# Cross-attention and ternary FFN on one core: attention scores as sixteen 32-row products with a key tile two heads wide

## The chip, the cores and the metric

The kernel runs as one program on one core of a Trainium2 chip. The metric is device time in microseconds (us) of one execution; lower is better. Three executions of the kernel before took 215.14 us in the median (214.61 to 218.46).

## What is computed

x is 8 batches of 256 tokens by 256 features; the context has 8 batches of 64 keys by 64 features. The first half is cross-attention with 16 heads of 16 features:

```
n = layernorm(x)
q = n @ Wq.T;  k, v = split(ctx @ Wkv_expand.T)
scores[b,h] = q[b,h] @ k[b,h].T / sqrt(16)      # 256 queries x 64 keys
scores = where(tril(256 x 64), scores, -max)    # only queries below 64 are masked
out = softmax(scores) @ v;  x = x + out @ Wout.T
```

The second half is a gated FFN on layernorm(x): rms-normalised and rounded activations, ternary weights, `silu(x w1) * (x w2)` (1024 wide), again rounded, times w3, added to x.

## The kernel before

Each engine has its own instruction list, written by hand, and waits on semaphores; nothing reorders it. The attention of one batch b is handled in steps that the lists spread over several iterations, so that the five engines work on different batches at once. The attention part is `iteration(0)` to `iteration(6)` (3 and 4 in a hardware loop), after a preamble that loads and transposes the weights and starts batches 0 to 2; after it come 16 token blocks of the FFN.

The steps around the change, for one batch b, with the engine's name (PE is TensorE, DVE VectorE, ACT ScalarE, POOL GpSimd):

- `keys(b)`, POOL, L334: builds the tile `k_diag`. For each of two chunks c of 128 features (8 heads of 16) it holds 8 heads x 64 keys = 512 columns; column block h is the keys' features times a 0/1 mask `head_of` that leaves only head h's 16 rows. Chunk 1 of batch 0 is built by DVE instead (L1000).
- `scores(b)`, PE: two matmuls of 512 columns add the causal mask to the first 128 queries' scores (L502). Then for each half t of the queries and each chunk c one fp32 matmul of 128 rows by 512 columns (L511): `wide[n*512:...]` with n = 2t + c, one PSUM bank each. After each half it signals `scores_done`. An fp32 matmul appears in the trace as two records, so these four are x8.
- `maximum(b, t)`, DVE, L942: row maximum per head of half t, once that half's scores are signalled. `shift(b, t)`, L948: subtracts it and writes `probs`. Both read 1024 columns, two whole banks.
- ACT: exponentials of `probs` (L779); POOL: `half_sums` (L366); DVE: `sums` (L955) and the reciprocal; PE: transposes of `probs` (`probs_T`, L462), `weigh` (L536, eight fp32 matmuls on four 32-column groups of the array, x16 in the trace), `recip_T`; DVE: `divide` (L963); PE: `project` (L555); DVE: `residual` (L969).

`qT` (the projected queries, features on partitions) and `kT` have features in the order of `Wq` and `Wkv_expand`, which PE transposes at the start (`square_T`, and the four wkv transposes).

Orders that the prediction speaks of. DVE in iteration j: `sums(j)`, `divide(j-1)`, `measure(j+3)`, `maximum(j+1, 0)`, ..., `residual(j-1)`, `maximum(j+1, 1)`, two `shift(j+1)`. PE in iteration j: `scores(j+1)`, `probs_T(j, 0)`, from j = 3 `tokens_T(j-3)` (L615, transposes of the FFN's quantised tokens, which ACT writes in L819), `project(j-1)`, `probs_T(j, 1)`, `query(j+2)`, `weigh(j)`, `recip_T(j)`, `normT(j+3)`. In the preamble PE has `values_of(0)`, `values_of(2)`, `scores(0)`, `values_of(4)`, `values_of(6)` (L477), `normT(1)` (L462), `query(1)`, and then the sum of the weights' magnitudes (L663) that DVE waits for.

Of the kernel before, what the change touches and what calls it, by code (L numbers as in the profile page):

```python
# [19 lines left out]
bf16 = mybir.dt.bfloat16  # L20
i16 = mybir.dt.int16
ALU = mybir.AluOpType
ACT = mybir.ActivationFunctionType
AX = mybir.AxisListType

P = 128
# [10 lines left out]
def need(engine, semaphore, value):  # L37

    if isinstance(value, int) and value <= 0:
        return  # L40
    engine.wait_ge(semaphore, value)


def build_program(nc, x_d, ctx_d, wq_d, wkv_d, wout_d, w1_d, g1_d, w2_d, g2_d, w3_d, g3_d, out_d):
    B, S, D = x_d.shape
    SK, L = ctx_d.shape[1:]
    H = w1_d.shape[0]
    NH = 16
    HD = D // NH
    TB = S // P  # L50
    DC = D // P
    HC = H // P
    HPC = NH // DC
    PR = HPC // 2
# [6 lines left out]
    with stack:  # L61
        def sb(name, shape, dt=fp32):
            return stack.enter_context(nc.sbuf_tensor(name, shape, dt))
# [4 lines left out]
        def sem(name):  # L68
            return stack.enter_context(nc.semaphore(name))
# [3 lines left out]
        wq_in = sb("wq_in", [P, DC, D])  # L73
        wout_in = sb("wout_in", [P, DC, D])
        wkv_in = sb("wkv_in", [P, 2 * DC, L])
# [5 lines left out]
        ident_h = sb("ident_h", [P, P], bf16)  # L81
        ones = sb("ones", [P, P])
        mask_h = sb("mask_h", [P, HPC, SK], bf16)
        head_of = sb("head_of", [P, HPC])
        key_half = sb("key_half", [P, 2])
        wqT = sb("wqT", [P, DC, D])
# [3 lines left out]
        kT = sb("kT", [P, DC, B * SK])  # L90
        v_all = sb("v_all", [P, B, D])
        k_diag = sb("k_diag", [P, DC, HPC, SK])
        v_pair = sb("v_pair", [P, 2 * PR, 2, HD])
# [10 lines left out]
        qT = sb("qT", [P, DC, S])  # L104
        row_max = sb("row_max", [P, TB, NH])
# [40 lines left out]
            "scores_done", "max_ready", "shifted", "probs_ready", "sums_ready", "recip_ready"))  # L146
        recip_wide, kp0_ready, half_ready = sem("recip_wide"), sem("kp0_ready"), sem("half_ready")
        pT_done, pT_ready, pv_done, rT_done, rT_ready, attnT_ready = map(sem, (
# [102 lines left out]
        with nc.Block() as block:  # L251
# [32 lines left out]
            def _(pool):  # L284
# [19 lines left out]
                g.affine_select(out=mask_h[:], in_=mask_h[:], compare_op=ALU.is_ge, fill=MASKED, base=0,  # L304
                                pattern=[[0, HPC], [-1, SK]], channel_multiplier=1).then_inc(const_set, 1)

# [22 lines left out]
                def keys(b):  # L329

                    need(pool, scores_done, 2 * b)

                    for c in range(1 if isinstance(b, int) and b == 0 else DC):
                        last = g.tensor_tensor(  # L334
                            out=k_diag[:, c, :, :],
                            in0=kT[:, c, bass.ds(b * SK, SK)].unsqueeze(1).to_broadcast([P, HPC, SK]),
                            in1=head_of[:].unsqueeze(2).to_broadcast([P, HPC, SK]), op=ALU.mult)
                    last.then_inc(kp_ready, 1)

# [10 lines left out]
                norm(0)  # L350
                pool.wait_ge(kT_set, 2)
                keys(0)
                pool.wait_ge(v_set, 1)
# [106 lines left out]
            def _(pe):  # L460
                def transpose(out, in_, n=P):
                    return nc.tensor.matmul(out, in_, ident[0:n, 0:n], is_transpose=True, start=True, stop=True)  # L462

                pe.wait_ge(ident_set, 1)

                def square_T(bank_, w):

                    for kc in range(DC):
                        for oc in range(DC):
                            last = transpose(bank_[:, (kc * DC + oc) * P:(kc * DC + oc + 1) * P],  # L470
                                             w[:, oc, kc * P:(kc + 1) * P])
                    return last
# [25 lines left out]
                def scores(b):  # L498

                    need(pe, shifted, 2 * b)  # L500
                    for c in range(DC):
                        nc.tensor.matmul(wide[:, c * 512:(c + 1) * 512], ident_h[:], mask_h[:],  # L502
                                         start=True, stop=False)
                    need(pe, qT_ready, b + 1)
                    need(pe, kp_ready, b + 1)
                    if isinstance(b, int) and b == 0:
                        pe.wait_ge(kp0_ready, 1)
                    for t in range(TB):
                        for c in range(DC):
                            n = t * DC + c  # L510
                            last = nc.tensor.matmul(wide[:, n * 512:(n + 1) * 512], qT[:, c, t * P:(t + 1) * P],  # L511
                                                    k_diag[:, c, :, :], start=(t == 1), stop=True)
                        last.then_inc(scores_done, 1)

# [65 lines left out]
                pe.wait_ge(wq_ld, 16)  # L580
                square_T(bank7, wq_in).then_inc(wqT_done, 1)
                keep_warm(5)
# [5 lines left out]
                pe.wait_ge(wkv_ld, 16)  # L588
                for n in range(2 * DC):
                    last = transpose(wide[0:L, n * P:(n + 1) * P], wkv_in[:, n, :])  # L590
# [150 lines left out]
            def _(act):  # L741
# [14 lines left out]
                def query_copy(b):  # L756
                    need(act, q_done, b + 1)
                    need(act, scores_done, 2 * b)
                    a.copy(qT[:].rearrange("p c s -> p (c s)"), bank5[:]).then_inc(qT_ready, 1)
# [158 lines left out]
            def _(dve):  # L918
# [17 lines left out]
                def by_head(ap, t):  # L936

                    return ap[:].rearrange("p (t n k) -> p t n k", t=TB, k=SK)[:, t, :, :]

                def maximum(b, t):  # L940
                    need(dve, scores_done, 2 * b + t + 1)
                    v.tensor_reduce(out=row_max[:, t, :], in_=by_head(wide, t), op=ALU.max,  # L942
                                    axis=AX.X).then_inc(max_ready, 1)

                def shift(b, t):
                    need(dve, max_ready, 2 * b + t + 1)
                    need(dve, pT_done, 4 * b - 2 + 2 * t if not isinstance(b, int) or b else 0)
                    v.tensor_tensor(probs[:, t, :].rearrange("p (n k) -> p n k", k=SK), by_head(wide, t),  # L948
                                    row_max[:, t, :].unsqueeze(2).to_broadcast([P, NH, SK]),
                                    ALU.subtract).then_inc(shifted, 1)  # L950
# [25 lines left out]
                def weights_T_copy(i, half):  # L976
# [4 lines left out]
                dve.wait_ge(ident_set, 1)  # L981
                v.tensor_copy(ident_h[:], ident[:]).then_inc(cast_set, 1)
                dve.wait_ge(x0_in, 16)
                measure(0)
# [12 lines left out]

                dve.wait_ge(const_set, 3)
                dve.wait_ge(kT_set, 2)
                v.tensor_tensor(k_diag[:, 1, :, :], kT[:, 1, 0:SK].unsqueeze(1).to_broadcast([P, HPC, SK]),  # L1000
                                head_of[:].unsqueeze(2).to_broadcast([P, HPC, SK]), ALU.mult).then_inc(kp0_ready, 1)

# [308 lines left out]
```

## Time and profile before

| | |
|---|---|
| median of 3 executions | 215.14 us (214.61 to 218.46) |
| profiled execution: span from first to last instruction (the only time shown for it) | 215.0 us |
| DVE busy | 184.2 us (86%) |
| PE busy | 170.9 us (79%) |
| ACT busy | 152.4 us (71%) |
| POOL busy | 143.6 us (67%) |
| mean granted TensorE clock | 0.959 of full speed |

The profile comes from one profiled execution. Its busy times add up what each engine was occupied; a PE record's end is modelled, so that successive records overlap, and a busy PE need not be one at its peak. The granted clock has two levels here: 1.00 is 2.4 GHz, 0.50 is 1.2 GHz. A timeline row gives the start, the time covered and, in brackets, how long the engine sat idle before the row and which engine, tile and line ended the idle time. Idle time counts only where the idle engine is the one that the end waits for.

### The profile page before, as it was taken

How to read it: one execution, taken by the hardware profiler on the slowest of the kernel's cores; microseconds unless marked ns; L12 is line 12 of the kernel's file. 1: busy time of each engine (PE TensorE's matmuls, PEld its weight loads, DVE VectorE, ACT ScalarE, POOL GpSimd, SP SyncE). 2: the span in 40 equal slices, each digit the busy share in tenths (PEclk: the TensorE clock that was granted, in tenths of full speed). 3: DMA queues.
4: the chain of work that ended last, by engine and by line, in shares of the span. 5: the costliest groups of instructions: out<-in, count | busy, mean ns of one | idle time of the engine just before them, and what ended most of it. 6: DMA issues, size and time to landing. Idle time of an engine off the chain costs nothing.

```text
span 215.0 us, 3666 instructions
## 1 busy us (share of the span) xinstructions
PE 170.9 (79%) x1073; PEld 110.0 (51%) x1080; DVE 184.2 (86%) x338; ACT 152.4 (71%) x218; POOL 143.6 (67%) x229
## 2 busy tenths in 40 slices
PE   4799877998997998999948878447489978788372
PEld 4755545585674865747436545124236544454251
DVE  2359799599999899997995889799999999999981
ACT  2355888958665896859864998829499968877622
POOL 5216292555667696886461666879899999999640
PEclk9999999999999999999997999959969999999979
DMA  6999000000000000000000000000000100010011
GB/s 163 340 377 361 27 3 2 0 2 5 0 0 3 0 0 0 0 0 3 2 0 0 0 3 0 0 2 0 30 24 24 49 24 24 24 52 24 24 49 49
DMA packets 8798, 9.09 MB, mean 42 GB/s; under 512 B 1488, under 2 KB 8400, under 8 KB 8784
## 3 DMA queue, kind: packets, MB, share of 16 engines
q1 hardware_dynamic: 8512, 8.65, 12.4%
q10 hardware_dynamic: 272, 0.26, 0.4%
q8 instruction: 7, 0.11, 0.2%
q14 instruction: 7, 0.06, 0.1%
HBM read 6.82 MB, written 2.10 MB: 41 GB/s over the span
## 4 chain that ended last, share of the span: by engine, by line
DVE 38%; issue 21%; PE 16%; ACT 12%; POOL 10%; DMA 2%; DVEq 1%; POOLq 0%; ACTq 0%
DVE hh L1195 5%; DVE probs L948 4%; DVE c_max L1213 4%; ACT q_x L819 4%; POOL u L384 4%; PE bank L555 3%; PE wide L511 3%; DVE m_x L1066 3%; DVE u_max L1059 3%; PE bank L706 2%; POOL half_sum L366 2%; DVE row_sum L955 2%; ACT hT L880 2%; DVE row_max L942 2%; PE bank L494 2%
## 5 line engine op out<-in xcount | busy, mean ns | idle before, releaser
L687 PE MATMUL wide<-wT,xqT 128*128 128x512 bf16 x128 | 33.5, 406 | 5.7 <-DVE hh L1195 3.5
L404 POOL TENSOR_TENSOR c_h<-hh,g3b 128x1024 f32<-128x1024 f32 x15 | 35.4, 2361 | 2.9 <-DVE hh L1195 2.5
L511 PE MATMUL wide<-k_diag,qT 128*128 128x512 f32 x64 | 28.9, 595 | 0.3 <-DVE k_diag L1000 0.3
L875 ACT ACTIVATE sq_junk<-hh,root_x 128x1024 bf16<-128x1024 f32 x16 | 18.4, 1147 | 15.2 <-DVE hh L1195 15.2
L706 PE MATMUL bank<-wT,hT 128*128 128x256 bf16 x128 | 17.6, 283 | 11.8 <-ACT hT L880 11.8
L334 POOL TENSOR_TENSOR k_diag<-kT,head_of 128x512 f32<-128x512 f32 x15 | 15.4, 1045 | 12.6 <-DVE kT L996 7.3
L819 ACT ACTIVATE q_x<-u,round_c,qs_x 128x256 f32<-128x256 f32 x32 | 16.6, 590 | 9.4 <-issue 5.1
L384 POOL TENSOR_TENSOR u<-xc,g 128x512 f32<-128x512 f32 x16 | 20.3, 1290 | 4.4 <-ACT q_x L819 4.4
L687 PEld LDWEIGHTS wide<-wT,xqT 128*128 128x128 bf16 (+1 forms) x128 | 12.3, 102 | 20.6 <-issue 7.3
L366 POOL TENSOR_TENSOR half_sum<-probs 128x512 f32<-128x512 f32 x16 | 20.1, 1277 | 3.4 <-ACT probs L779 3.3
L706 PEld LDWEIGHTS bank<-wT,hT 128*128 128x128 bf16 x128 | 11.6, 100 | 20.5 <-ACT hT L880 16.8
L764 ACT COPY probsT<-bank 128x512 f32<-128x512 f32 x32 | 17.1, 588 | 6.7 <-PE bank L462 6.5
L880 ACT ACTIVATE hT<-bank,round_c 128x1024 bf16<-128x1024 int16 x16 | 17.6, 1100 | 4.4 <-PE bank L615 4.4
L942 DVE TENSOR_REDUCE row_max<-wide 128x16 f32<-128x1024 f32 x16 | 19.5, 1217 | 0.9 <-PE wide L511 0.5
L1195 DVE TENSOR_TENSOR hh<-gate,wide 128x1024 f32<-128x1024 f32 x16 | 19.4, 1210 | 0.1
L1213 DVE TENSOR_REDUCE c_max<-c_h 128x1 f32<-128x1024 f32 x16 | 19.3, 1208 | 0.0
L511 PEld LDWEIGHTS wide<-k_diag,qT 128*128 128x128 f32 x64 | 12.0, 190 | 13.5 <-issue 12.2
L948 DVE TENSOR_TENSOR probs<-wide,row_max 128x1024 f32<-128x1024 f32 x16 | 18.7, 1213 | 0.0
L462 PE MATMUL bank<-ident,probs 128*128 128x128 f32 x128 | 16.7, 273 | 2.2 <-ACT probsT L764 1.4
L462 PEld LDWEIGHTS bank<-ident,probs 128*128 128x128 f32 x128 | 14.8, 142 | 7.0 <-issue 6.1
L869 ACT ACTIVATE gate<-wide,dq_x 128x1024 f32<-128x1024 f32 x16 | 17.8, 1110 | 0.4 <-PE wide L687 0.4
L555 PE MATMUL bank<-woutT,attnT 128*128 128x256 f32 x64 | 17.0, 414 | 0.7 <-DVE attnT L963 0.7
(139 smaller groups left out, 385.8 us busy)
## 6 DMA issues: line engine op xcount, KB each, us to landing
w_in<-in_L_ffn_w SPq DMA_DIRECT2D x3, 1024.0 KB, 10.3
out<-y SPq DMA_DIRECT2D x16, 128.0 KB, 1.7
x_sb<-in_x SPq DMA_DIRECT2D x1, 1280.0 KB, 12.4
x_sb<-in_x SPq DMA_DIRECT2D x1, 512.0 KB, 5.3
g3b<-in_L_ffn_g SPq DMA_DIRECT2D x1, 512.0 KB, 7.9
wq_in<-in_L_xattn_Wq ACTq DMA_DIRECT2D x1, 256.0 KB, 4.0
x_sb<-in_x SPq DMA_DIRECT2D x1, 256.0 KB, 3.6
wout_in<-in_L_xattn_Wout SPq DMA_DIRECT2D x1, 256.0 KB, 12.2
```

The costliest lines, as they stand in the source:

```text
L366: last = g.tensor_tensor(out=half_sum[:, t, :, :], in0=e[:, :, 0, :], in1=e[:, :, 1, :], op=ALU.add)
L384: last = g.tensor_tensor(out=u[:, t, :, :], in0=xc[:, t, :].unsqueeze(1).to_broadcast([P, 2, D]), in1=g12[:], op=ALU.mult)
L404: g.tensor_tensor(out=c_h[:, t, :], in0=hh[:, t, :], in1=g3b[:], op=ALU.mult).then_inc(c_ready, 1)
L462: return nc.tensor.matmul(out, in_, ident[0:n, 0:n], is_transpose=True, start=True, stop=True)
L511: last = nc.tensor.matmul(wide[:, n * 512:(n + 1) * 512], qT[:, c, t * P:(t + 1) * P], k_diag[:, c, :, :], start=(t == 1), stop=True)
L687: last = nc.tensor.matmul(wide[:, (w * 2 + n) * 512:(w * 2 + n + 1) * 512], xqT_cols(T, w * DC + c), w_cols[:, 4 * n:4 * n + 4, c, :], sta ...
L706: last = nc.tensor.matmul(down_banks[t][:, 0:D], hT[:, t, n, :], w_cols[:, n, :, :], start=(n == 0), stop=(n == HC - 1))
L819: last = a.activation(q_x[:, t, w, :], u[:, t, w, :], ACT.Identity, scale=qs_x[:, t, w:w + 1], bias=round_c[:, 0:1])
L942: v.tensor_reduce(out=row_max[:, t, :], in_=by_head(wide, t), op=ALU.max, axis=AX.X).then_inc(max_ready, 1)
L948: v.tensor_tensor(probs[:, t, :].rearrange("p (n k) -> p n k", k=SK), by_head(wide, t), row_max[:, t, :].unsqueeze(2).to_broadcast([P, NH, ...
L1195: v.tensor_tensor(hh[:, t, :], gate[:, t, :], wide[:, H:2 * H], ALU.mult).then_inc(hh_ready, 1)
L1213: v.tensor_reduce(out=c_max[:, t:t + 1], in_=c_h[:, t, :], op=ALU.max, axis=AX.X, apply_absolute_value=True).then_inc(cm_ready, 1)
```

## The change

The scores of one batch become sixteen fp32 matmuls instead of four. The features of `Wq` and of the keys' part of `Wkv_expand` are permuted while they are transposed (`by_chunk`), so that the 32 rows of row group r in chunk c hold heads 4r + 2c and 4r + 2c + 1. Each matmul takes 32 rows of one group, 128 queries and 128 columns (2 heads x 64 keys), and writes to bank r; the four that follow each other use the four row groups and four banks. The key tile `k_pair` needs a 0/1 mask for two heads only (`half_of`, built once by DVE), and has 2 x 128 columns instead of 2 x 512. It is built by one POOL instruction a batch, also for batch 0, where the DVE instruction L1000 goes. The mask of the scores goes to four banks with 256 columns each. Each bank now holds both halves t, so `scores_done` is signalled once, after all sixteen, and `maximum(b, 0)` waits for that; the waits of `query_copy` and `keys` on it are counted accordingly. `maximum` and `shift` read a half as four pieces of 256 columns in the four banks, again 1024 columns.

```diff
@@ keys (POOL)
-                    need(pool, scores_done, 2 * b)
-
-                    for c in range(1 if isinstance(b, int) and b == 0 else DC):
-                        last = g.tensor_tensor(
-                            out=k_diag[:, c, :, :],
-                            in0=kT[:, c, bass.ds(b * SK, SK)].unsqueeze(1).to_broadcast([P, HPC, SK]),
-                            in1=head_of[:].unsqueeze(2).to_broadcast([P, HPC, SK]), op=ALU.mult)
-                    last.then_inc(kp_ready, 1)
+                    need(pool, scores_done, b)
+                    g.tensor_tensor(
+                        out=k_pair[:], in0=kT[:, :, bass.ds(b * SK, SK)].unsqueeze(2).to_broadcast([P, DC, 2, SK]),
+                        in1=half_of[:].unsqueeze(1).unsqueeze(3).to_broadcast([P, DC, 2, SK]),
+                        op=ALU.mult).then_inc(kp_ready, 1)
@@ transposes of wq and wkv (PE)
+                def by_chunk(ap, block):
+
+                    at = ap.rearrange("p (c r k) -> p r c k", c=DC, k=2 * HD)
+                    return at[:, block * PR // DC:(block + 1) * PR // DC, :, :]
...
@@ scores (PE)
-                    for c in range(DC):
-                        nc.tensor.matmul(wide[:, c * 512:(c + 1) * 512], ident_h[:], mask_h[:],
-                                         start=True, stop=False)
+                    for r in range(PR):
+                        nc.tensor.matmul(wide[:, r * 512:r * 512 + 2 * P], ident_h[:], mask_h[:],
+                                         start=True, stop=True)
                     need(pe, qT_ready, b + 1)
                     need(pe, kp_ready, b + 1)
-                    if isinstance(b, int) and b == 0:
-                        pe.wait_ge(kp0_ready, 1)
                     for t in range(TB):
                         for c in range(DC):
-                            n = t * DC + c
-                            last = nc.tensor.matmul(wide[:, n * 512:(n + 1) * 512], qT[:, c, t * P:(t + 1) * P],
-                                                    k_diag[:, c, :, :], start=(t == 1), stop=True)
-                        last.then_inc(scores_done, 1)
+                            for r in range(PR):
+                                rows, at = slice(32 * r, 32 * r + 32), r * 512 + (t * DC + c) * P
+                                last = nc.tensor.matmul(wide[:, at:at + P], qT[rows, c, t * P:(t + 1) * P],
+                                                        k_pair[rows, c, :, :], start=(t == 1), stop=True,
+                                                        skip_group_check=True)
+                    last.then_inc(scores_done, 1)
@@ maximum and shift (DVE)
-                    return ap[:].rearrange("p (t n k) -> p t n k", t=TB, k=SK)[:, t, :, :]
+                    return ap[:].rearrange("p (r t n k) -> p r t n k", r=PR, t=TB, k=SK)[:, :, t, :, :]
...
-                    need(dve, scores_done, 2 * b + t + 1)
+                    need(dve, scores_done, b + 1)
@@ DVE, preamble
+                dve.wait_ge(const_set, 3)
+                v.tensor_reduce(out=half_of[:], in_=head_of[:].rearrange("p (r h) -> p h r", h=2), op=ALU.add,
+                                axis=AX.X).then_inc(half_of_set, 1)
...
-                dve.wait_ge(const_set, 3)
-                dve.wait_ge(kT_set, 2)
-                v.tensor_tensor(k_diag[:, 1, :, :], kT[:, 1, 0:SK].unsqueeze(1).to_broadcast([P, HPC, SK]),
-                                head_of[:].unsqueeze(2).to_broadcast([P, HPC, SK]), ALU.mult).then_inc(kp0_ready, 1)
```

On PE, in the preamble from the first values to the second ones, the order of instructions before (the last numbers are an instruction's rows by columns):

```order
L477 MATMUL bank<-wkvT,ctxT 128x256 x4
L502 MATMUL wide<-mask_h,ident_h 128x512 x2
L511 MATMUL wide<-k_diag,qT 128x512 x4
L477 MATMUL bank<-wkvT,ctxT 128x256 x4
L462 MATMUL bank<-ident,nrm 128x128 x4
```

and in the change:

```order
L480 MATMUL bank<-wkvT,ctxT 128x256 x4
L505 MATMUL wide<-mask_h,ident_h 128x256 x4
L513 MATMUL wide<-k_pair,qT 128x128 x16
L480 MATMUL bank<-wkvT,ctxT 128x256 x4
L461 MATMUL bank<-ident,nrm 128x128 x4
```

The place of the scores in the list is the same, here and in every iteration; two masks and four products have become four and sixteen, with as many columns in all for the masks (1024) and for the products (2048).

On DVE, the start of its list, before:

```order
L982 CAST ident_h<-ident 128x128
L927 BN_STATS ln_bn<-x_sb 128x6 x2
L933 BN_AGGR ln_mv<-ln_bn 128x2 x2
L988 TENSOR_SCALAR wqT<-bank 128x512
L991 COPY ctxT<-bank 64x1024
L994 COPY wkvT<-wide 64x512
L996 COPY kT<-wide 128x512
L1000 TENSOR_TENSOR k_diag<-kT,head_of 128x512
L1005 COPY v_all<-bank 128x512 x2
```

and in the change:

```order
L991 CAST ident_h<-ident 128x128
L993 TENSOR_REDUCE half_of<-head_of 128x2
L932 BN_STATS ln_bn<-x_sb 128x6 x2
L938 BN_AGGR ln_mv<-ln_bn 128x2 x2
L1000 TENSOR_SCALAR wqT<-bank 128x512
L1003 COPY ctxT<-bank 64x1024
L1006 COPY wkvT<-wide 64x512
L1008 COPY kT<-wide 128x512
L1013 COPY v_all<-bank 128x512 x2
```

The key instruction between the copy of the keys and the copies of the values is gone; a reduction to two columns stands near the start.

## Rows read from the trace of the kernel before

**Rows 1.** The page: busy time, share of the span and instructions by engine.

```profile
PE 170.9 (79%) x1073; PEld 110.0 (51%) x1080; DVE 184.2 (86%) x338; ACT 152.4 (71%) x218; POOL 143.6 (67%) x229
```

**Rows 2.** Groups by line: busy us, mean ns of one; idle before, releaser.

```profile
L511 PE MATMUL wide<-k_diag,qT 128*128 128x512 f32 x64 | 28.9, 595 | 0.3 <-DVE k_diag L1000 0.3
L942 DVE TENSOR_REDUCE row_max<-wide 128x16 f32<-128x1024 f32 x16 | 19.5, 1217 | 0.9 <-PE wide L511 0.5
L1213 DVE TENSOR_REDUCE c_max<-c_h 128x1 f32<-128x1024 f32 x16 | 19.3, 1208 | 0.0
L334 POOL TENSOR_TENSOR k_diag<-kT,head_of 128x512 f32<-128x512 f32 x15 | 15.4, 1045 | 12.6 <-DVE kT L996 7.3 <-PE wide L511 5.1
L344 POOL TENSOR_TENSOR v_pair<-v_all,key_half 128x256 f32<-128x256 f32 x8 | 4.9, 618 | 12.6 <-PE bank L536 11.4 <-DVE v_all L1005 1.2
```

**Rows 3.** Timeline of the preamble, all engines: start us, us covered.

```profile
13.47 1.89 PE L477 MATMUL bank<-wkvT,ctxT 64*128 64x256 f32 x8
14.44 1.04 POOL L334 TENSOR_TENSOR k_diag<-kT,head_of 128x512 f32<-128x512 f32 x1 [7.29 <-DVE kT L996]
14.47 1.56 DVE L1000 TENSOR_TENSOR k_diag<-kT,head_of 128x512 f32<-128x512 f32 x1
15.95 1.27 DVE L1005 COPY v_all<-bank 128x512 f32<-128x512 f32 x2
16.18 3.67 PE L511 MATMUL wide<-k_diag,qT 128*128 128x512 f32 x8 [0.28 <-DVE k_diag L1000]
18.26 0.19 POOL L320 TENSOR_TENSOR ln_ve<-ln_mv,ln_eps 128x2 f32<-128x2 f32 x1 [0.94 <-DVE ln_mv L933]
19.78 1.99 PE L477 MATMUL bank<-wkvT,ctxT 64*128 64x256 f32 x8
19.82 1.09 ACT L748 ACTIVATE nrm<-x_sb,ln_nb,ln_rstd 128x256 f32<-128x256 f32 x2 [1.77 <-POOL ln_nb L327]
21.03 2.35 DVE L948 TENSOR_TENSOR probs<-wide,row_max 128x1024 f32<-128x1024 f32 x2
21.70 0.66 PE L462 MATMUL bank<-ident,nrm 128*128 128x128 f32 x4
25.43 0.16 DVE L1031 TENSOR_SCALAR w_s<-bank 128x3 f32<-128x3 f32 x1 [1.39 <-PE bank L663]
```

**Rows 4.** Windows, iterations 2 and 4: length, busy PE, PEld, DVE, ACT, POOL, PEclk, ...

```profile
56.70:70.75 14.05, 12.35 (x82) 8.54 (x82) 13.64 (x28) 8.68 (x15) 9.94 (x14) 1.00 0.01 1
83.86:96.55 12.69, 11.76 (x73) 8.11 (x74) 12.27 (x26) 9.94 (x17) 9.69 (x15) 1.00 0.00 0
```

**Rows 5.** Timeline of iterations 1 and 3: PE, ACT, DVE.

```profile
40.45 3.60 PE L511 MATMUL wide<-k_diag,qT 128*128 128x512 f32 x8
44.70 1.22 DVE L942 TENSOR_REDUCE row_max<-wide 128x16 f32<-128x1024 f32 x1
67.36 3.60 PE L511 MATMUL wide<-k_diag,qT 128*128 128x512 f32 x8
69.36 2.07 ACT L819 ACTIVATE q_x<-u,round_c,qs_x 128x256 f32<-128x256 f32 x4 [2.42 <-DVE qs_x L1087]
74.23 0.69 DVE L969 TENSOR_TENSOR x_sb<-bank,x_sb 128x512 f32 x1 [0.67 <-PE bank L555]
```

**Rows 6.** Timeline, PE: the column-group products of one batch (`weigh`).

```profile
89.11 1.07 PE L536 MATMUL bank<-probsT,v_pair 128*32 128x256 f32 x16
```

**Rows 7.** Windows around 112 us (columns as above), and timeline of two projects.

```profile
108.50:111.90 3.40, 0.78 (x8) 0.47 (x8) 3.19 (x14) 2.46 (x5) 1.51 (x2) 1.00 0.00 0
111.90:115.30 3.40, 3.23 (x8) 2.60 (x9) 1.25 (x2) 2.22 (x4) 1.69 (x2) 0.50 0.00 0
...
84.63 1.95 PE L555 MATMUL bank<-woutT,attnT 128*128 128x256 f32 x8
112.07 3.58 PE L555 MATMUL bank<-woutT,attnT 128*128 128x256 f32 x8 [0.67 <-DVE attnT L963]
115.69 0.69 DVE L969 TENSOR_TENSOR x_sb<-bank,x_sb 128x512 f32<-128x512 f32 x1 [2.54 <-PE bank L555]
```

More of the change, by code:

```diff
@@ L82, in build_program @@
         ones = sb("ones", [P, P])
-        mask_h = sb("mask_h", [P, HPC, SK], bf16)
+        mask_h = sb("mask_h", [P, 2 * DC, SK], bf16)
         head_of = sb("head_of", [P, HPC])
+        half_of = sb("half_of", [P, 2])
         key_half = sb("key_half", [P, 2])
@@ L91, in build_program @@
         v_all = sb("v_all", [P, B, D])
-        k_diag = sb("k_diag", [P, DC, HPC, SK])
+        k_pair = sb("k_pair", [P, DC, 2, SK])
         v_pair = sb("v_pair", [P, 2 * PR, 2, HD])
@@ L146, in build_program @@
             "scores_done", "max_ready", "shifted", "probs_ready", "sums_ready", "recip_ready"))
-        recip_wide, kp0_ready, half_ready = sem("recip_wide"), sem("kp0_ready"), sem("half_ready")
+        recip_wide, half_of_set, half_ready = sem("recip_wide"), sem("half_of_set"), sem("half_ready")
         pT_done, pT_ready, pv_done, rT_done, rT_ready, attnT_ready = map(sem, (
@@ L304, in _ @@
                 g.affine_select(out=mask_h[:], in_=mask_h[:], compare_op=ALU.is_ge, fill=MASKED, base=0,
-                                pattern=[[0, HPC], [-1, SK]], channel_multiplier=1).then_inc(const_set, 1)
+                                pattern=[[0, 2 * DC], [-1, SK]], channel_multiplier=1).then_inc(const_set, 1)
                 g.affine_select(out=head_of[:], in_=head_of[:], compare_op=ALU.is_ge, fill=0.0, base=0,
@@ L351, in _ @@
                 pool.wait_ge(kT_set, 2)
+                pool.wait_ge(half_of_set, 1)
                 keys(0)
@@ L464, in _, with square_T @@
                 pe.wait_ge(ident_set, 1)
-                def square_T(bank_, w):
+                def by_chunk(ap, block):
+                    at = ap.rearrange("p (c r k) -> p r c k", c=DC, k=2 * HD)
+                    return at[:, block * PR // DC:(block + 1) * PR // DC, :, :]
+                def square_T(bank_, w, place=lambda ap, block: ap[:, block * P:(block + 1) * P]):
                     for kc in range(DC):
                         for oc in range(DC):
-                            last = transpose(bank_[:, (kc * DC + oc) * P:(kc * DC + oc + 1) * P],
-                                             w[:, oc, kc * P:(kc + 1) * P])
+                            last = transpose(place(bank_[:, kc * D:(kc + 1) * D], oc), w[:, oc, kc * P:(kc + 1) * P])
                     return last
@@ L580, in _ @@
                 pe.wait_ge(wq_ld, 16)
-                square_T(bank7, wq_in).then_inc(wqT_done, 1)
+                square_T(bank7, wq_in, by_chunk).then_inc(wqT_done, 1)
                 keep_warm(5)
@@ L588, in _ @@
                 pe.wait_ge(wkv_ld, 16)
-                for n in range(2 * DC):
+                for n in range(DC):
+                    transpose(by_chunk(wide[0:L, 0:D], n), wkv_in[:, n, :])
+                for n in range(DC, 2 * DC):
                     last = transpose(wide[0:L, n * P:(n + 1) * P], wkv_in[:, n, :])
@@ L757, in query_copy @@
                     need(act, q_done, b + 1)
-                    need(act, scores_done, 2 * b)
+                    need(act, scores_done, b)
                     a.copy(qT[:].rearrange("p c s -> p (c s)"), bank5[:]).then_inc(qT_ready, 1)
@@ L936, in by_head, with by_pair @@
                 def by_head(ap, t):
-                    return ap[:].rearrange("p (t n k) -> p t n k", t=TB, k=SK)[:, t, :, :]
+                    return ap[:].rearrange("p (r t n k) -> p r t n k", r=PR, t=TB, k=SK)[:, :, t, :, :]
+                def by_pair(ap):
+                    return ap.rearrange("p (r n) -> p r n", r=PR)
                 def maximum(b, t):
-                    need(dve, scores_done, 2 * b + t + 1)
-                    v.tensor_reduce(out=row_max[:, t, :], in_=by_head(wide, t), op=ALU.max,
+                    need(dve, scores_done, b + 1)
+                    v.tensor_reduce(out=by_pair(row_max[:, t, :]), in_=by_head(wide, t), op=ALU.max,
                                     axis=AX.X).then_inc(max_ready, 1)
@@ L947, in shift @@
                     need(dve, pT_done, 4 * b - 2 + 2 * t if not isinstance(b, int) or b else 0)
-                    v.tensor_tensor(probs[:, t, :].rearrange("p (n k) -> p n k", k=SK), by_head(wide, t),
-                                    row_max[:, t, :].unsqueeze(2).to_broadcast([P, NH, SK]),
+                    v.tensor_tensor(probs[:, t, :].rearrange("p (r n k) -> p r n k", r=PR, k=SK), by_head(wide, t),
+                                    by_pair(row_max[:, t, :]).unsqueeze(3).to_broadcast([P, PR, 2 * DC, SK]),
                                     ALU.subtract).then_inc(shifted, 1)
```

## The prediction

> **What bounds the kernel now.** I read the busy shares first: DVE is the fullest engine, 184.2 of 215.0 us, and PE follows with 170.9 [rows 1]. A share is an average, so the windows come next. In iterations 2 and 4 of the attention DVE is busy 13.64 of 14.05 us and 12.27 of 12.69, and PE, whose records overlap, 12.35 and 11.76 [rows 4]. The reader is to see there that what shortens an iteration is DVE work, or a wait of DVE; PE time counts only where DVE waits for PE. The groups by line tell where it does: DVE's row maxima had 0.5 us of idle before them that ended with the scores, in the whole run, and the scores cost PE 28.9 us [rows 2]. So nearly all of the scores' time lies beside DVE work. In the iterations, the other wait of DVE on PE is for `project`: 0.67 us in iteration 3 [rows 5] and 2.54 us in iteration 6 [rows 7].
>
> The preamble is different. There the engines wait for each other in a chain that passes through the scores of batch 0: PE's scores end at 19.85 us, the second values (1.99 us) run until 21.77, and `normT(1)`, ready since ACT's normalisation ended at 20.91, goes behind them at 21.70. DVE waits 1.39 us, until 25.43, for the weights' sum, and that sum comes from ACT and PE work behind `normT(1)` [rows 3].
>
> **The scores on PE.** An L511 record streams 512 columns; eight take 3.60 us, of which the last one's length is 0.59 [rows 2, 5], so a record's pace is (3.60 - 0.59) / 7 = 0.43 us, and 0.107 us for 128 columns. The change has 32 records of 128 columns, the same 4096 columns in all. How fast they go on four row groups the trace doesn't show. Bounds: one after another, 32 x 0.107 = 3.4 us and a last record's tail, no gain; four at a time, a quarter, 0.86 us, and a tail. The nearest row is `weigh`: 16 records of 256 columns, again 4096, on four column groups take 1.07 us [rows 6]. I take that, and 0.2 us more for twice as many, shorter records and for changing from whole-array to row-group products: **1.3 us** a batch, 2.3 less than now. The masks cover 1024 columns as before: nothing.
>
> The Trainium skill (page "TensorE: Matmul & The Clock Gate", Part 3) gives 3.07 times for four 32-row groups with 512 columns. By that the stage would be 3.6 / 3.07 = 1.17 us, an estimate from the page; no row of this trace has row groups.
>
> **The preamble.** DVE no longer builds half the key tile: 1.56 us go [rows 3]. It goes straight to the two value copies, 1.27 us, but the second must wait for PE's values, which end at 15.36, so the copies end near 16.1 instead of 17.2, and the statistics of batch 1 are ready near 17.1, 1.1 us earlier. POOL's one key instruction writes 256 columns; `v_pair` with as many takes 0.618 us [rows 2], so it is ready at 14.44 + 0.62 = 15.06. PE is through with values at 15.36 and with the masks near 15.95; the scores start there, only 0.2 us earlier than now, and end near 17.3 instead of 19.85. The second values end at 19.3. `normT(1)` then waits no more for PE: POOL's norm (18.26 to 19.79 before) and ACT's 1.09 us [rows 3] start 1.1 us earlier, so it starts at 19.8 instead of 21.70. That is 1.9 us. I count **1.8 us**, since some copies sit between. Behind it come the last magnitude sum on ACT, the weights' sum on PE, the query copy and exponentials of batch 0, half sums and row sums, each released by the one before, so the whole attention starts 1.8 us earlier. DVE must be ready too: maxima from 17.4 (instead of two starts with a wait between), shifts done at 21.9 instead of 23.38: it is. `half_of` is a small reduction in DVE's idle start: nothing.
>
> **The iterations.** The maxima wait for the whole batch, not for a half. Behind `maximum(j+1, 0)` on DVE stand `residual(j-1)`, the second maximum and both shifts, so a wait there would be paid in full. But the scores end ahead: in iteration 1 at 44.05, with all eight records, and the first maximum starts at 44.70; in iteration 3 at 70.96 (67.36 + 3.60) [rows 5]. With 1.3 us the reserve grows to about 3 us. The wait costs nothing, and its cover is gone only when the stage takes over 4.2 us.
>
> What do 2.3 us less of PE give? In iteration 3, `project(2)` stands behind the transposes of tokens, and those behind ACT's quantising, which ends at 69.36 + 2.07 = 71.43. PE comes to them after the scores, which end at 70.96, and eight transposes of `probs`, so later than ACT; then it would be there first and wait for ACT. Project and residual gain between nothing and the 0.67 us that DVE waits [rows 5]; I take 0.4, a little over the middle, because the last token transposes still stand behind 71.43. In iterations 4 and 5 the tokens already set the start of project, in 6 the quotient from DVE does (the row of project at 112.07 names it [rows 7]): nothing. **0.4 us** in all. POOL's keys go from 2 x 1.045 to about 0.62 us, 1.47 us less a batch [rows 2]. POOL isn't full in the windows (9.94 and 9.69 us [rows 4]), and next in its list it waits for statistics from DVE: nothing. `maximum` and `shift` read as many columns; DVE's reduction with 16 results (1217 ns) costs 9 ns more than one with a single result (1208 ns) [rows 2], so the shape of a pattern is worth at most 32 x 0.01 = 0.3 us, which I leave to the range. The FFN is not touched.
>
> **Sum:** 215.0 - 1.8 - 0.4 = 212.8 us of span. The median of the runs shown is 0.1 us above that span, so **212.9 us**, 1.0% less. A measurement of this kernel tells a change from none at about 2%, or 4.3 us. This case has 60%, and its own range is 211.8 to 214.0.
>
> **Rivals.**
> - *The row groups don't overlap* (17%). Each record needs its own weights, 128 columns wide; `weigh` loads 32 columns [rows 6] and doesn't show that wide loads go beside each other. Then scores(0) ends near 15.95 + 3.5 = 19.5, `normT(1)` gains 0.3 us, iteration 3 nothing: 214.8 us. The Trainium skill (same page, section "LDWEIGHTS (loading the stationary operand)") has a load's time go by its columns, rows not counting; 32 loads one after another would be 32 x 128 / 1.2 ns = 3.4 us, an estimate, and lead to this case.
> - *A lower clock* (13%). At 111.9 us the granted clock fell to 0.50 (1.2 GHz) after a stretch in which PE had been busy 0.78 of 3.40 us; project then took 3.58 us instead of 1.95, and DVE waited 2.54 us for it [rows 7]. Shorter scores leave PE idle about 2 us ahead of the tokens in iterations 4 and 5. If the clock falls there too, each costs about 1.6 us: 214.5 to 216.1.
> - *Slower: weight loads that nothing hides* (6%). If a record can't start before its own load ends, the pace goes from 0.107 to, say, twice that (load and stream alike): 32 x 0.214 = 6.9 us, 3.3 more than now. The point from which it decides is 4.2 us a batch, 0.13 us a record, where the first maximum in iteration 1 starts to wait. Beyond it DVE pays 3.3 us less a reserve of 0.65 to 1.2 in each of iterations 1 to 3, I guess 2 us in the later ones together, and the preamble 3: 7 + 2 + 3 = 12, so 227 us. Against it: L511's loads, as wide, are started under the running record, with no gap in the pace.
> - *More than forecast* (4%): DVE instructions held up by POOL's (L1000 took 1.56 us for what POOL did in 1.04 [rows 3]) get shorter as POOL has less to do, in the iterations too; up to 3 us more: 209.8.
>
> The range of 8 in 10 takes in the first case, the second and most of the third: 211.5 to 216.0. Faster by over 2%: the last case and a bit, 0.05. Slower by over 2%: the unhidden loads and several falls of the clock, 0.08. Within 2%: 0.87.
>
> **What the profile after would show.** The new L513 group: 32 records in about 1.3 us a batch if the groups overlap (10 us in all instead of 28.9), 3.5 if not. `normT(1)` near 19.8 us, the weights' sum on DVE near 23.6 instead of 25.43. The first maximum without idle time that the scores end. Iterations as long as before (14.0 and 12.7 us), with PE idle in place of scores. Wrong would be: a maximum that waits for L513; iterations shorter by more than 0.5 us each, which would say that PE, not DVE, bounds them; or stretches at clock 0.50 before 100 us.

## The result, and the profile after

The changed kernel takes 220.35 us in the median of 4 executions (218.69 to 221.42), the kernel before beside it 214.88 (214.60 to 218.46). The ratio is 1.026, with a 95% interval of 1.019 to 1.032: slower. All ratios here are of the executions that lie within about 1.5% of their kernel's fastest. I had forecast 212.9 us, 211.5 to 216.0. Only three executions of the kernel before stand in this ratio (214.60 to 215.14). In 75 later ones, on the chips of the experiments, it took 214.34 to 219.88 us, 217.35 in the median. Against those the change's four are about 3 us slower, not 5.5: that it is slower holds, the size of the loss is less sure than the interval says. The profiled execution's span is 219.6 us, 4.6 more than before.

The page of the changed kernel: busy time by engine, and the granted clock in 40 slices.

```profile
PE 166.0 (76%) x1288; PEld 115.3 (53%) x1288; DVE 182.7 (83%) x338; ACT 152.8 (70%) x218; POOL 132.3 (60%) x222
PEclk9998888999999995896975999758889999999955
```

The same line of the kernel before:

```profile
PEclk9999999999999999999997999959969999999979
```

The groups of the new lines (busy us, mean ns of one, idle before):

```profile
L513 PE MATMUL wide<-k_pair,qT 32*128 32x128 f32 x256 | 9.4, 283 | 0.1
L513 PEld LDWEIGHTS wide<-k_pair,qT 32*128 32x128 f32 x256 | 7.9, 186 | 1.9 <-issue 1.5 <-ACT qT L764 0.4
L333 POOL TENSOR_TENSOR k_pair<-kT,half_of 128x256 f32<-128x256 f32 x8 | 4.9, 614 | 7.3 <-DVE kT L1008 7.3
```

The scores cost 9.4 us of PE in all instead of 28.9 [rows 2], the key tiles 0.614 us each: both as priced. What the reader is to see are the two lines of the clock. In the kernel before it stays up from the start-up to 111.9 us [rows 7]; now windows of half a microsecond show it lowered from 20.7, 30.9, 82.1, 99.2 and 112.8 us on, and in the FFN. Stretches at 0.50 before 100 us were what the prediction had named as a sign of being wrong.

The changed kernel's timeline in the preamble:

```profile
15.74 1.17 PE L513 MATMUL wide<-k_pair,qT 32*128 32x128 f32 x32
16.85 1.99 PE L480 MATMUL bank<-wkvT,ctxT 64*128 64x256 f32 x8
19.73 0.66 PE L461 MATMUL bank<-ident,nrm 128*128 128x128 f32 x4 [0.89 <-ACT nrm L753]
21.06 3.48 PE L497 MATMUL bank<-nT,wqT 128*128 128x256 f32 x8 [0.68 <-ACT nT L759]
24.77 0.16 DVE L1039 TENSOR_SCALAR w_s<-bank 128x3 f32<-128x3 f32 x1 [2.50 <-PE bank L668]
```

`normT(1)` starts at 19.73 instead of 21.70 [rows 3], where I had put it at 19.8. But `query(1)` then takes 3.48 us; before, the same eight records took 1.99. Of 2.0 us gained 0.66 are left at the weights' sum (24.77 against 25.43).

Windows of the changed kernel (length, then busy PE, PEld, DVE, ACT, POOL, the granted clock third from last): for two of the falls the stretch before it, and the one at the low clock behind it.

```profile
17.00:20.60 3.60, 2.49 (x12) 1.68 (x12) 3.60 (x4) 2.23 (x5) 1.85 (x5) 1.00 1.12 356
20.80:24.00 3.20, 2.94 (x7) 2.40 (x8) 1.46 (x3) 2.11 (x3) 0.00 (x0) 0.50 0.36 138
77.50:82.00 4.50, 2.68 (x45) 2.02 (x42) 4.13 (x12) 2.44 (x5) 3.59 (x6) 1.00 0.00 0
82.20:88.90 6.70, 6.11 (x24) 5.02 (x25) 4.49 (x10) 4.11 (x8) 3.19 (x7) 0.50 0.00 0
```

And the kernel before in the same stretch of iteration 4:

```profile
77.50:82.00 4.50, 4.45 (x21) 2.58 (x19) 4.36 (x13) 2.84 (x4) 3.67 (x6) 1.00 0.00 0
```

PE was busy 4.45 of 4.50 us there before, 2.68 now, and the clock goes to 0.50 (1.2 GHz). The timeline of the changed kernel shows what that costs:

```profile
82.42 0.60 PE L620 MATMUL bank<-ident_h,q_x 128*128 128x128 bf16 x4 [2.06 <-ACT q_x L824]
83.80 3.73 PE L558 MATMUL bank<-woutT,attnT 128*128 128x256 f32 x8
87.69 0.69 DVE L978 TENSOR_TENSOR x_sb<-bank,x_sb 128x512 f32 x1 [2.05 <-PE bank L558]
101.55 0.69 DVE L978 TENSOR_TENSOR x_sb<-bank,x_sb 128x512 f32<-128x512 f32 x1 [2.20 <-PE bank L558]
```

The time that the shorter scores give back turns up as 2.06 us of idle PE in front of the tokens' transposes. `project` then runs at half the clock, 3.73 us instead of 1.95 [rows 7], and DVE waits 2.05 us for it, in an iteration in which it had not waited for it at all. In iteration 5 the wait is 2.20 us where it was 1.13, in iteration 6 2.75 (2.54 before [rows 7]).

By the starts of DVE's row sums (batches 0, 4, 5, 6, 7), and of the last gated product of the FFN, the 4.6 us come about like this:

| | before | after | difference |
|---|---|---|---|
| row_sum 0 | 30.26 | 29.75 | -0.5 |
| row_sum 4 | 82.33 | 81.33 | -1.0 |
| row_sum 5 | 95.02 | 96.06 | +1.0 |
| row_sum 6 | 109.87 | 112.19 | +2.3 |
| row_sum 7 | 124.23 | 126.87 | +2.6 |
| last hh (L1195, L1203) | 200.94 | 203.50 | +2.6 |
| end | 215.0 | 219.6 | +4.6 |

The last 2.0 us are the tail: there the clock is at 0.50 from 208.4 us on, and `down` takes 1.89 us, twice:

```profile
210.89 1.89 PE L711 MATMUL bank<-wT,hT 128*128 128x256 bf16 x8 [1.21 <-ACT hT L885]
214.84 1.89 PE L711 MATMUL bank<-wT,hT 128*128 128x256 bf16 x8 [1.21 <-ACT hT L885]
```

Before, one of the last three took 1.89 and two 1.05. The FFN's code is unchanged, and PE is idle in the same places; when the clock falls there differs between executions. The profile of e9 below, a run with the FFN and the scores of the kernel before, has such a tail too: clock 0.50 from 206.8 us on, `down` at 1.89 us in its last two places, and 15.7 us from the last hh to the end, where the two kernels above have 14.1 and 16.1. So a tail like this needs no change in the scores, and these 2.0 us are not shown to be the change's.

### The profile page after: what moved, and what is told of

Its sections match the earlier page's. It is cut to its first block, busy times and chain, and to the rows that moved or that the text cites. A ratio compares the mean times of both kernels' runs of the same rounds, so it can differ in the third digit from the quotient of the medians.

```text
span 219.6 us, 4080 instructions
## 1 busy us (share of the span) xinstructions
PE 166.0 (76%) x1288; PEld 115.3 (53%) x1288; DVE 182.7 (83%) x338; ACT 152.8 (70%) x218; POOL 132.3 (60%) x222
## 4 chain that ended last, share of the span: by engine, by line
DVE 37%; PE 18%; issue 18%; ACT 13%; POOL 10%; DMA 2%; DVEq 1%; POOLq 0%; ACTq 0%
PE bank L558 6%; DVE hh L1203 5%; POOL u L383 5%; DVE probs L957 4%; DVE c_max L1221 4%; ACT q_x L824 4%; DVE u_max L1067 4%; PE bank L497 3%; DVE m_x L1074 3%; PE bank L461 3%; PE bank L711 2%; DVE row_sum L964 2%; DVE xc L1061 2%; ACT hT L885 2%; DVE fb_bn L1048 2%
## 5 line engine op out<-in xcount | busy, mean ns | idle before, releaser
L692 PE MATMUL wide<-wT,xqT 128*128 128x512 bf16 x128 | 34.1, 411 | 4.5 <-DVE hh L1203 3.1
L711 PE MATMUL bank<-wT,hT 128*128 128x256 bf16 x128 | 18.4, 292 | 12.0 <-ACT hT L885 12.0
L558 PE MATMUL bank<-woutT,attnT 128*128 128x256 f32 x64 | 20.3, 473 | 3.2 <-DVE attnT L972 3.2
L824 ACT ACTIVATE q_x<-u,round_c,qs_x 128x256 f32<-128x256 f32 x32 | 16.6, 590 | 8.7 <-DVE qs_x L1095 4.5
L461 PE MATMUL bank<-ident,probs 128*128 128x128 f32 x128 | 20.5, 311 | 1.7 <-ACT nT L759 1.0
L461 PEld LDWEIGHTS bank<-ident,probs 128*128 128x128 f32 x128 | 17.4, 163 | 5.1 <-issue 3.1
L1203 DVE TENSOR_TENSOR hh<-gate,wide 128x1024 f32<-128x1024 f32 x16 | 19.4, 1211 | 0.1
L321 POOL TENSOR_TENSOR ln_ve<-ln_mv,ln_eps 128x2 f32<-128x2 f32 x8 | 1.6, 194 | 29.7 <-DVE ln_mv L938 29.7
L558 PEld LDWEIGHTS bank<-woutT,attnT 128*128 128x128 f32 x64 | 14.3, 235 | 6.4 <-DVE attnT L972 4.2
L497 PE MATMUL bank<-nT,wqT 128*128 128x256 f32 x64 | 16.8, 409 | 0.7 <-ACT nT L759 0.7
```

Source lines behind the costliest of these rows:

```text
L497: last = nc.tensor.matmul(bank5[:, oc * S:(oc + 1) * S], wqT[:, kc, oc * P:(oc + 1) * P], nT[:, kc, :], start=(kc == 0), stop=(kc == DC - 1))
L558: last = nc.tensor.matmul(bank4[:, t * D:(t + 1) * D], attnT[:, c, t * P:(t + 1) * P], woutT[:, c, :], start=(c == 0), stop=(c == DC - 1))
L692: last = nc.tensor.matmul(wide[:, (w * 2 + n) * 512:(w * 2 + n + 1) * 512], xqT_cols(T, w * DC + c), w_cols[:, 4 * n:4 * n + 4, c, :], sta ...
L711: last = nc.tensor.matmul(down_banks[t][:, 0:D], hT[:, t, n, :], w_cols[:, n, :, :], start=(n == 0), stop=(n == HC - 1))
L824: last = a.activation(q_x[:, t, w, :], u[:, t, w, :], ACT.Identity, scale=qs_x[:, t, w:w + 1], bias=round_c[:, 0:1])
L1203: v.tensor_tensor(hh[:, t, :], gate[:, t, :], wide[:, H:2 * H], ALU.mult).then_inc(hh_ready, 1)
```

## The experiments

All are compared with the kernel before in executions on the same chip; the changed kernel itself was not run again beside them, so that a ratio here and its 1.026 come from different sets. Theory: the idler PE loses its clock, and each fall makes longer what runs in it. Rivals: the row groups or the banks, the wait for the whole batch, or POOL and DVE in each other's way.

**More PE work in front of the scores (e1_mask7).**

```diff
-                    for r in range(PR):
+                    for r in list(range(PR)) * 7:
                         nc.tensor.matmul(wide[:, r * 512:r * 512 + 2 * P], ident_h[:], mask_h[:],
```

> The changed kernel with each batch's four mask products issued seven times over (24 more whole-array products of 256 bf16 columns, the same values written again; about 2.6 us of PE work a batch, as much as the change took away). Theory (the clock): the row-group products are fine, 1.17 us a batch; what is lost comes from stretches at clock 0.50 that the idler PE brings. Then the mean clock goes back from 0.89 to 0.95 or more and the time from 220.35 to about that of the kernel before or a little less, 212.5 to 215. Rival (the work): the loss lies in the new order of waits or in POOL and DVE work getting into each other's way; then 2.6 us more of PE work a batch gives nothing back, and the time stays at 219 to 222. Rival (the kind of work): row-group products themselves lower the clock; then it stays below 0.93 too.

Measured: ratio to the kernel before 1.002 (0.998 to 1.007), span 215.4 us, clock 0.966, no fall before 112 us:

```profile
PEclk9999999999999999999997999979969999999979
```

With 2.6 us of useless work more a batch the changed kernel takes 217.23 us in the median of 12, where it had taken 220.35, and the loss against the kernel before is gone. It is not faster than the kernel before: in the preamble the masks stand in the chain, the scores of batch 0 start at 19.05 us instead of 15.74, and row_sum 0 at 30.63.

**The same with row-group work (e2_rowpass3).** Before the masks, the sixteen products run twice with `start=True`; their results are overwritten.

```diff
+                    def products(extra):
...
+                    products(True)
+                    products(True)
                     for r in range(PR):
                         nc.tensor.matmul(wide[:, r * 512:r * 512 + 2 * P], ident_h[:], mask_h[:],
                                          start=True, stop=True)
...
+                    last = products(False)
```

> The changed kernel with the sixteen row-group products of a batch issued three times (two passes whose results are overwritten, then masks and the real pass): 2.3 us more PE work a batch, all of it in 32-row products. Theory (the clock goes by how much PE works, whatever the rows): like the kernel with seven masks, mean clock 0.95, 212.5 to 216 us. Rival (row-group products count for less than whole-array ones): the clock stays near 0.90 and the time at 218 us or more, since this one has the same time of work as the seven masks but in 32-row pieces.

Measured: 0.992 (0.987 to 0.997), span 214.0, clock 0.959, no fall before 111 us. So 32-row products on four groups hold the clock too; the rival on their kind falls. Row sums start 0.7 to 1.0 us ahead of the kernel before all through the attention: what is left of the preamble's gain.

**Shorter scores without row groups (e3_bf16).** The kernel before with scores of lower precision:

```diff
-        k_diag = sb("k_diag", [P, DC, HPC, SK])
+        k_diag = sb("k_diag", [P, DC, HPC, SK], bf16)
...
-        qT = sb("qT", [P, DC, S])
+        qT = sb("qT", [P, DC, S], bf16)
```

> The kernel before with qT and k_diag in bf16, so that the scores lose precision: four whole-array products of 512 columns at one pass each, about 0.9 us a batch instead of 3.6, with the old banks, the old wide key tile and the old signals. Theory (an idler PE lowers the clock): it falls in the iterations as in the changed kernel, mean clock about 0.90, and the time is 217 to 221 us although PE has 2.7 us less to do a batch. Rival (the fault lies in row groups, banks or the wait for the whole batch): the clock stays at 0.95 and the time is 212 to 214.5.

Measured: 1.020 (1.013 to 1.028), span 219.0, clock 0.905: slower, like the change. Its page and its iteration 4:

```profile
PEclk9998585999999997896975999957969999999969
80.65 1.03 PE L511 MATMUL wide<-k_diag,qT 128*128 128x512 bf16 x4
...
85.28 0.58 PE L615 MATMUL bank<-ident_h,q_x 128*128 128x128 bf16 x4 [2.07 <-ACT q_x L819]
86.67 2.98 PE L555 MATMUL bank<-woutT,attnT 128*128 128x256 f32 x8
89.81 0.69 DVE L969 TENSOR_TENSOR x_sb<-bank,x_sb 128x512 f32 x1 [1.29 <-PE bank L555]
```

Old banks, old key tile, old signals, and the same picture: short scores, 2.07 us idle, `project` at 2.98 us, DVE waiting. So the loss needs neither the row groups nor the new banks, key tile or signals. Its place is another in part, though: e3's clock is at 0.50 from 20.5 to 27.3 us and from 30.7 to 37.6, twice as long as the change's first two falls, and its row sums of batches 0 and 1 start 1.5 and 2.4 us later than before, that of batch 7 4.0 us later.

**The wait alone (e4_wait_both).**

```diff
-                    need(dve, scores_done, 2 * b + t + 1)
+                    need(dve, scores_done, 2 * b + 2)
```

> The kernel before in which the first maximum also waits for the second half of the scores; nothing else is changed. Theory: outside batch 0 the scores end at least 0.6 us before the first maximum starts, so 214.9 us, within 0.3%; batch 0's maxima come 1.4 us later, but DVE waits there later for the weights' sum anyway. Rival (the wait for a whole batch costs the change its time): each iteration longer by 0.5 us or more, 218 to 220.

Measured: 0.999 (0.993 to 1.005), span 214.9, the row sums where they were. No cost of the wait for the batch shows, even with the long scores. (In e4's preamble DVE waits 0.27 us for the weights' sum instead of 1.39, which takes up the later maxima, as expected.)

**Filling the idle time itself.** The filler is a whole-array product of 256 bf16 columns into a bank that PE overwrites next. In the preamble:

```diff
+                fill(bank6[:, 0:2 * P], 8)
                 normT(1)
+                fill(bank5[:, 0:2 * P], 6)
                 query(1)
...
                         pe.wait_ge(inv_ready, 1)
+                        fill(bank6[:, 0:2 * P], 20)
                         normT(2)
```

and in the iterations:

```diff
                     probs_T(j, 0)
+                    if from_(j, 1):
+                        need(pe, rT_ready, j)
+                        fill(bank5[:, 0:2 * P], 24 if isinstance(j, int) and j == 6 else 14 if from_(j, 3) else 11)
```

> The changed kernel with idle PE time filled in the preamble only (34 whole-array products of 256 bf16 columns before normT(1), query(1) and normT(2), into banks that these then overwrite). Theory (idle PE lowers the clock, and each fall costs what runs in it): no fall before 80 us, query(1) back from 3.48 to 2.0 us, row sums of batch 0 at 28.3 instead of 29.75 us; the falls at 82, 99 and 113 us stay. 1.4 us less than the changed kernel: 218 to 220 us in the same company. Rival (the falls follow the row-group products): falls near 21 and 31 us stay.

> The changed kernel with the idle time of iterations 1 to 6 filled, behind probs_T(j, 0), where PE waits for ACT's tokens or DVE's quotient (11 products of 256 bf16 columns in iterations 1 and 2, 14 in 3 to 5, 24 in 6). Theory: the falls at 82, 99 and 113 us go, DVE's waits for project in iterations 4 to 6 go back from 2.05, 2.20 and 2.75 us to 0, 1.1 and 0.9, together 3.5 us or more less than the changed kernel: 215 to 217 us. Rival (the fill is in the way, since PE has no room before project): iterations as long as in the changed kernel.

> The changed kernel with both fills, preamble and iterations. Theory: the two effects add up, 4.9 us or more less than the changed kernel, 1.5 to 2.5 us less than the kernel before; clock 0.95 or more, falls only in the FFN. Rival: the preamble's gain is lost again in the iterations, no better than with the iterations' fill alone.

| | ratio (95%) | median of all | span | clock | row_sum 0 | row_sum 7 |
|---|---|---|---|---|---|---|
| before | 1 | 217.32 (23) | 215.0 | 0.959 | 30.26 | 124.23 |
| after, in its own set | 1.026 (1.019 to 1.032) | 220.35 (4) | 219.6 | 0.889 | 29.75 | 126.87 |
| e5, preamble | 1.005 (1.000 to 1.010) | 217.44 (12) | 214.4 | 0.943 | 28.86 | 123.75 |
| e6, iterations | 0.983 (0.975 to 0.992) | 215.68 (6) | 211.4 | 0.966 | 28.88 | 120.72 |
| e7, both | 0.984 (0.977 to 0.990) | 212.74 (6) | 212.3 | 0.965 | 29.01 | 120.86 |

e5 has no fall before 94 us, e7 none before 136. In e6's profile the first fall comes at 29.7 us instead of 20.7, behind `query(1)`, so it got the preamble's gain without a fill there, with the preamble's code of the changed kernel. In the profiles the effects do not add up, against what I had expected of e7. Over all executions they differ: e6's ratio rests on three of six, and the other three took 218.17 to 220.78 us with a mean clock of 0.915 to 0.943, and no profile shows where the clock fell in them; e7's six took 212.35 to 215.35, at 0.965 or more. So only e7's gain is there each time.

e5 did better than I expected, and for a reason that the theory lacks. I had the fall at 82 us stay; it is gone, though PE is idle in iteration 4 as long as in the changed kernel:

```profile
81.51 0.40 PE L627 MATMUL bank<-ident_h,q_x 128*128 128x128 bf16 x4 [2.06 <-ACT q_x L832]
82.73 1.95 PE L563 MATMUL bank<-woutT,attnT 128*128 128x256 f32 x8
```

`project` runs at the full clock and DVE does not wait for it; the falls come at 94.6 and 108.3 us. So an idle stretch of 2.06 us is followed by a fall in one profile and not in another, and what decides it is left open. e7's profile: its clock, and iterations 4 and 6:

```profile
PEclk9999999999999999999999999859979999999978
79.45 1.69 PE L480 MATMUL bank<-mask_h,ident_h 128*128 128x256 bf16 x14
...
82.89 1.95 PE L563 MATMUL bank<-woutT,attnT 128*128 128x256 f32 x8
110.29 1.99 PE L563 MATMUL bank<-woutT,attnT 128*128 128x256 f32 x8 [0.67 <-DVE attnT L983]
112.32 0.69 DVE L989 TENSOR_TENSOR x_sb<-bank,x_sb 128x512 f32<-128x512 f32 x1 [0.96 <-PE bank L563]
```

Fourteen products lie in what had been idle time, `project` takes 1.95 us again, DVE does not wait in iteration 4 and waits 0.96 us instead of 2.54 in iteration 6. This version beats both kernels: 212.74 us in the median of 6, beside 217.32 for the kernel before.

**A third of the fill (e10_fill_half):** e7 with 4, 5 and 8 products in place of 11, 14 and 24.

> The changed kernel with the preamble's fill and a third of the iterations' fill (4 products in iterations 1 and 2, 5 in 3 to 5, 8 in 6). Theory (the clock asks for a certain amount of work, and a little of it may be missing): between the preamble's fill alone and the full fill; a fall near 109 us stays, those near 82 and 95 us may go: 214 to 217 us. Rival (any products at all in the gap hold the clock): as fast as with the full fill.

Measured: 1.006 (1.002 to 1.011), span 216.6, falls at 96.1 and 109.8 us: no better than the preamble's fill alone. In these gaps some work did not do: iteration 5 has five products and a fall at 96.1 us, and DVE waits 2.82 us in it. As in e5, iteration 4 has no fall.

**The fill on the kernel before (e9_before_fill6):** 24 products, in iteration 6 only.

> The kernel before with idle PE time filled in iteration 6 only (24 whole-array products of 256 bf16 columns behind probs_T(6, 0)), where its own fall of the clock at 112 us begins. It tells how much of the gain of the filled changed kernel is the fill alone. Theory: DVE's wait for project falls from 2.54 to 0.9 us, 1.6 us less than the kernel before; the filled changed kernel's other 1.2 us are the shorter scores' and the preamble's. Rival (all of the gain is the fill): as fast as the filled changed kernel, 2.7 us less than the kernel before.

Measured: 1.001 (0.995 to 1.006). Its profile shows the 1.6 us in iteration 6 (DVE waits 0.96 us), but falls near 138, 156 and from 207 us to the end, and a span of 216.8. The time does not show the gain, so the times can't say how e7's 1.6% divides between fill and change; that the fill of iteration 6 alone does not make it is what this run supports. The profiles divide the attention's part. From DVE's copy of the keys (`kT`) to row_sum 7 the kernel before takes 110.6 us, e9 109.0, e7 106.6: of 4.0 us, 1.6 are the fill in iteration 6, and 2.4 come before it, from the change with its clock held.

**Fill in the FFN (e8_fill_all, e11_fill_tail):** six products before each even `down` and each hidden transpose and 24 before the first; or only 24 before the first hidden transpose, and 10 and 6 in the last four blocks.

> As the kernel with both fills, and the FFN's waits of PE filled too (six products of 256 columns before each even down and before each transpose of a hidden tile, 24 before the first). Theory: the falls near 140, 157 and 205 us, which the kernel before has too, go or get fewer, 1.5 to 3 us less again: 3 to 5 us less than the kernel before. Rival: PE in the FFN is gated by DVE through hh, so that a lower clock there costs nothing outside the first blocks and the tail, and the fills delay the up products: no gain, or 1 us more.

> The filled changed kernel with the first hidden tile's wait and the last four blocks' waits filled too (10 products before down, 6 before the transposes). Theory: the falls near 136 and 201 us go and down in the tail takes 1.05 us instead of 1.89; each sits on the chain of the last blocks: 0.5 to 1.5 us less. Rival: the blocks' start is gated by POOL and DVE, the fill delays what comes behind: no change or 0.5 us more.

Measured: e8 0.995 (0.990 to 0.999), clock 1.000 with one fall in the last microsecond, span 212.0; e11 0.988 (0.981 to 0.995), clock 0.990, 211.7. Neither beats e7. With the full clock e8's FFN, from the first gated product at 122.4 us, takes 89.6 us; e7's, with falls, 89.2. A full clock bought with fills does not shorten the FFN. Whether the clock gives nothing there, or the fills take what it gives, these runs do not separate.

## Why the prediction was wrong

- **The step that failed** is the one that let 2.3 us less of PE in the iterations be worth "nothing" and no less than nothing. I priced the time and not what it had been holding up. The runs showed in its place that with PE idler the clock falls to 0.50: `project` in iteration 4 takes 3.73 us instead of 1.95, and DVE waits 2.05 us for it. The mechanism stood among the rivals as "a lower clock", with 13% and 214.5 to 216.1 us, too small a chance and too small a price: e3 brings a loss without the change, e1 and e2 take it away without undoing it. My list of DVE's waits for `project`, 0.67 and 2.54 us, also lacked the 1.13 us of iteration 5, where a slower `project` is paid for in full.
- Its size was short too. I counted falls in iterations 4 and 5 at 1.6 us each. Iteration 4 lost 2.0 and iteration 5 1.3, but the clock also fell in the preamble (`query(1)` 1.5 us longer), which I had not thought of, and the profiled execution had 2.0 us in the tail.
- **The scores on PE:** forecast 1.3 us, measured 1.17 (3.60 / 1.17 = 3.08 times). The Trainium skill (page "TensorE: Matmul & The Clock Gate", Part 3) gives 3.07 times for four row groups with 512 columns; the trace, with 128 columns, agrees. The Trainium skill's rule (same page, section "LDWEIGHTS (loading the stationary operand)") that a load's time goes by its columns does not make the loads of different row groups queue up: the 32 loads of a batch, 186 ns each, cover 7.9 us / 8 = 1.0 us together. Both rivals on weight loads fall.
- **The preamble:** 1.8 us forecast, 0.5 measured. The start-up differs between executions (the copy of `kT` starts at 13.5 to 14.7 us), so the stretch from that copy to row_sum 0 is the better measure: 16.6 us in the kernel before, in e4 and in e9, 16.2 in the change, and 14.7 in e5 to e8, e10 and e11, the six profiles with the change's own scores in which the clock stays up until past `query(1)`. That is 1.9 us less: the term was right at the full clock.
- **Iteration 3:** 0.4 us forecast for `project`; DVE's wait went from 0.67 to 0.30. Right. Once the clock is held (e7), the forecast's 1.8 + 0.4 = 2.2 us are there: 2.4 us by row_sum 4, from the copy of `kT`.
- **The wait for the whole batch** costs nothing that shows: right (e4). **POOL's shorter keys:** forecast nothing, and iterations 0 and 2 are as long as before. Iteration 1 is 0.27 us shorter, as DVE's `w_tern` takes 1.22 us instead of 1.48; in the kernel before POOL's keys run beside its start. That is a small piece of the rival "more than forecast".
- **The base of the sum.** I took the profiled execution to be 0.1 us off the median. In the later executions of the kernel before and in the change's the time is 1.7 to 1.8 us more than the span (221.29 for 219.6), and executions of the kernel before with the profiled one's span and clock took 216.7 us: the profiled execution was a slower one than the median of three that I started from. 212.9 is that median less 2.2 us, so the miss of 7.4 us is the 2.2 that did not come and 5.2 more. How much of the 5.2 comes from the few executions that both medians stand on is open; the profiles differ by 4.6 us, 2.0 of them in the tail.
- Still open: how far the tail's 2.0 us belong to the change, and why the idle stretch of iteration 4 is followed by a fall in the change and by none in e5.

## What to carry to other kernels

PE time that lies beside another engine's work may still hold PE's clock. Before such work is shortened, look where the idle time will end up, and what stands right behind it in PE's list: if that is on the chain, add a case in which it takes up to twice its length (here 1.95 us became 3.73). If the clock falls, cheap products into a bank that is about to be overwritten kept it up here: 34 in the preamble with 11 to 24 a gap in the iterations did (e7), with 4 to 8 a gap they did not (e10). They belong where PE waits anyway.

## What the runs showed of the hardware

- In the kernel before, too, time goes with the clock: the seven executions with a mean clock of 0.982 or 0.983 took 214.3 to 214.6 us, the fifteen with 0.959 took 216.5 to 218.1, the fourteen with 0.936 or 0.937 219.0 to 219.8. The mean clock does not settle it alone: the twenty with 0.966 or 0.967 took 215.0 to 217.6. One program is measured over several microseconds, and an average of few executions moves with its falls.
- A stretch need not be idle to be followed by a fall: from 17.0 to 20.6 us the changed kernel's PE records cover 2.49 of 3.60 us, with products of 64 rows and transposes of 128 columns. The Trainium skill (page "TensorE: Matmul & The Clock Gate", section "HAM oscillation — how this bites in real kernels") has idle gaps of PE between bursts bring the lower clock. The changed kernel's falls at 82 us, within a gap of 2.06 us, and at 99 us, 1.8 us behind a gap of 1.69 us, agree in kind; this stretch does so only in part, and in e5 a gap of 2.06 us brought no fall.
